# Experts' tiles of a routed mixture layer: three engines' programs turned from unrolled code into loops of four tiles

## The reference, cut to what matters

```python
logits = xt @ Wr + br                       # 4096 tokens of 128 values, 8 experts
top_p, top_idx = jax.lax.top_k(softmax(logits), 2)
xe = xn[None] * ln_g[:, None] + ln_b[:, None]
h = gelu(einsum('end,edh->enh', xe, W1) + b1[:, None], approximate=False)
y = einsum('enh,ehd->end', h, W2) + b2[:, None]
out = sum over the two chosen experts of weight * y
```

## Time and profile before

| | |
|---|---|
| median of the timed runs | 1002.8 us |
| the profiled execution, its span | 1045.3 us |
| share of the span by PE, DVE, ACT, POOL | 73%, 70%, 61%, 56% |
| matmuls | 7837 |
| instructions executed | 24181 |
| first tile's tokens to last tile's results | about 867 to 1007 us of the span |
| TensorE's granted clock there, in mid-stage | 1.00 |

### The profile page before, as it was taken

The page is one execution under the profiler, slowest core; times in us unless marked ns, Lnnn a source line. Parts: engine busy times, 40 slices in busy tenths (PEclk is TensorE's granted clock), DMA queues, the critical chain, the costliest instruction groups (busy, mean ns, idle before and its releaser), DMA issues. The chain is left out here.

```text
span 1045.3 us, 24181 instructions
## 1 busy us (share of the span) xinstructions
PE 761.2 (73%) x7837; PEld 473.6 (45%) x7837; DVE 729.2 (70%) x1821; ACT 641.5 (61%) x1446; POOL 587.3 (56%) x760
## 2 busy tenths in 40 slices
PE   2857888888888888888888599665554306899960
PEld 2444444444454454444544244212443305777750
DVE  2585788888888888888887715697745543666646
ACT  2656888887888888888888332285322404777740
POOL 0045777767767767767767499200065561555560
PEclk8896999999999999999999699888655557999995
DMA  9009999980000000000000050130011112222317
GB/s 218 1 2 203 172 187 118 6 3 0 0 0 0 0 0 0 0 0 0 0 0 0 4 159 1 55 126 3 1 41 41 33 44 60 64 83 73 83 47 241
DMA packets 109052, 54.07 MB, mean 52 GB/s; under 512 B 42688, under 2 KB 100824, under 8 KB 109008
## 3 DMA queue, kind: packets, MB, share of 16 engines
q1 hardware_dynamic: 102624, 43.34, 27.5%
q0 software_dynamic: 4544, 9.38, 2.8%
q10 hardware_dynamic: 1840, 0.79, 0.4%
HBM read 21.49 MB, written 29.44 MB: 49 GB/s over the span
## 5 line engine op out<-in xcount | busy, mean ns | idle before, releaser
L534 DVE SCALAR_TENSOR_TENSOR l_m<-l_m,l_eta,lp_g 128x256 f32<-128x256 f32 x512 | 219.6, 476 | 39.5 <-PE lp_g L646 26.0
L383 POOL TENSOR_TENSOR s_w<-l_kw,l_m 128x512 f32<-128x512 f32 x192 | 238.4, 1278 | 12.0 <-DVE l_m L534 12.0
L480 ACT ACTIVATE l_kw<-s_w,l_keep_lr 128x256 f32<-128x256 f32 x384 | 171.3, 507 | 0.0
L1338 POOL DMA_INDIRECT f_yg<-f_yr,f_xmeta x78 | 78.7, 1009 | 75.1 <-DVE f_yr L1668 55.9
L1333 POOL DMA_INDIRECT f_xg<-f_xrow,f_place x64 | 62.9, 983 | 74.7 <-DVE f_place L1564 56.4
L1313 ACT ACTIVATE f_hh<-fp_v,f_bcol 128x256 f32<-128x256 f32 x156 | 63.2, 480 | 33.4 <-PE fp_v L1433 32.4
L473 ACT COPY l_wt<-lp_b 128x512 f32<-128x512 f32 x96 | 56.4, 588 | 27.8 <-PE lp_b L639 27.8
L388 POOL TENSOR_TENSOR l_kw<-s_w,l_keep 128x512 f32<-128x512 f32 x64 | 65.2, 1040 | 0.0
L639 PE MATMUL lp_b<-s_cst,s_w 128*128 128x128 f32 x384 | 62.7, 287 | 2.3 <-ACT s_w L521 1.3
L1433 PE MATMUL fp_v<-f_xf,s_w_hi 128*128 128x256 bf16 x312 | 56.0, 281 | 9.3 <-DVE f_xmeta L1648 7.2
L639 PEld LDWEIGHTS lp_b<-s_cst,s_w 128*128 128x128 f32 x384 | 43.7, 143 | 32.5 <-ACT l_wt L473 13.8
(11 more groups left out here) (323 smaller groups left out, 2016.4 us busy)
## 6 DMA issues: line engine op xcount, KB each, us to landing
f_xg<-s_pad SPq DMA_DIRECT2D x1, 17280.0 KB, 106.7
f_xt<-f_xg SPq DMA_DIRECT2D x39, 130.0 KB
r_w<-in_L_ffn_W_dram SPq DMA_DIRECT2D x16, 256.0 KB, 3.1
s_w<-f_yg SPq DMA_DIRECT2D x16, 256.0 KB, 3.7
xs<-in_x_dram SPq DMA_DIRECT2D x8, 256.0 KB, 7.5
t_w<-in_L_ffn_W_dram SPq DMA_DIRECT2D x8, 256.0 KB
out_dram<-s_x SPq DMA_DIRECT2D x8, 256.0 KB, 3.0
s_xsh<-s_xl SPq DMA_DIRECT2D x4, 448.0 KB, 3.5
```

The lines of the kernel that those rows point to most:

```text
L383: nc.gpsimd.tensor_tensor(W[k][:, half(h), :], KW[k][:, half(h), :], M[k][:, half(h), :], ALU.add).then_inc(w_ready[k], 1)
L480: m = nc.scalar.mul(KW[k][:, b, :], W[k][:, b, :], keep_lr[:, b:b + 1])
L534: i = nc.vector.scalar_tensor_tensor(out=M[k][:, b, :], in0=M[k][:, b, :], scalar=eta[:, b:b + 1], in1=ps_g[b][:, 0:256], op0=ALU.mult, op ...
L1338: nc.gpsimd.indirect_dma_start(sb["yg"][:, :], bass.IndirectOffsetOnAxis(ap=xmeta[:, j, a, 0:1].bitcast(mybir.dt.int32), axis=0), yr[j % R ...
```

## The change

`RING` becomes 4. The fourth `f_hs` buffer, and all four of `f_yr`, are placed in the memory of `s_qf`, which is no longer used. The programs of TensorE, ScalarE and VectorE for the tiles are written as a helper `rounds`: tiles 0 to 5 stand written out, then a hardware loop of 8 rounds with four tiles in its body, then the rest (tile 38, and on TensorE and VectorE the two steps that drain the pipeline). Within the loop the number of the tile is a register expression, `at(r, k)`, so the numbers that are waited for, the column of `owneri` and the offsets of biases and of `xmeta` are computed in registers. TensorE reads the tile's owner twice, once for the first and once for the second layer, where before it kept the register. SyncE's and GpSimd's programs stay written out, with the ring of four. The order of the matmuls, activations and copies is as before. ScalarE's wait for a free `f_hs` buffer is for the second layer of three tiles ago as before; VectorE's is for that of four tiles ago.

```diff
-    RING = 3
+    RING = 4
+    AHEAD, ROUNDS = 6, 8
...
+        def at(r, k, n=1):
+            return r * (RING // n) + k // n
+
+        def rounds(engine, step, last):
+            for k in range(AHEAD):
+                step(0, k)
+            with engine.Fori(0, ROUNDS) as r:
+                for k in range(RING):
+                    step(r, AHEAD + k)
+            for k in range(AHEAD, last - RING * ROUNDS):
+                step(ROUNDS, k)
...
-                    if j >= 2:
-                        act.wait_ge(h_lo, 2 * (j - 1))
+                def activated(r, k):
+                    if k >= 2:
+                        act.wait_ge(h_lo, 2 * at(r, k - 1))
...
-                def owner_of(j):
-                    return nc.tensor.value_load(owner_i[0:1, j:j + 1], min_val=0, max_val=E - 1)
+                def owner_of(r, k):
+                    return nc.tensor.value_load(owner_i[0:1, bass.ds(at(r, k), 1)], min_val=0, max_val=E - 1)
...
+                def first_layer(r, k, e):
+                    pe.wait_ge(xf_ready, 2 * at(r, k) + 2)
+                    if k >= 2:
+                        pe.wait_ge(h_ready, NH * at(r, k - 1))
...
+                def layers(r, k):
+                    if RING * ROUNDS * (r is ROUNDS) + k + 1 < NJ:
+                        turn(r, k + 1)
+                    if RING * ROUNDS * (r is ROUNDS) + k < NJ:
+                        first_layer(r, k, owner_of(r, k))
+                    if k >= 2:
+                        second_layer(r, k - 2, owner_of(r, k - 2))
...
-                for j in range(NJ + 2):
-                    if j + 1 < NJ:
-                        turn(j + 1)
-                    if j < NJ:
-                        e = owners[j] = owner_of(j)
...
-                        e = owners.pop(i)
-                        pe.wait_ge(h_lo, 2 * (i + 1))
...
+                rounds(pe, layers, NJ + 2)
```

More of the change, by code:

```diff
@@ L1185, in experts @@
         spare = sb["qf"][:, :, :, :].rearrange("p b t c -> p (b t c)")
-        hs.append([spare[:, 512 * i:512 * i + 512].bitcast(BF16).rearrange("p (h n) -> p h n", h=NH) for i in range(2)])
-        yr = [buf(f"yr{i}", [128, 2, 128]) for i in range(RING)]
+        for n in range(2):
+            hs.append([spare[:, 1024 * n + 512 * i:1024 * n + 512 * i + 512].bitcast(BF16).rearrange("p (h n) -> p h n", h=NH) for i in range(2)])
+        yr = [spare[:, 2048 + 256 * i:2304 + 256 * i].rearrange("p (a n) -> p a n", a=2) for i in range(RING)]
         yb = [sb["w" + k][:, :, :].rearrange("p b n -> p (b n)").rearrange("p (k n f) -> p k n f", k=2, n=4) for k in ("10", "11", "21")]
@@ L1228, in tile_of, with plain @@
             return NTB * (i % B) + 2 * g + i // B
+        def at(r, k, n=1):
[8 more added lines that the diff above has]
+                step(ROUNDS, k)
+        def plain(step, last):
+            for k in range(last):
+                step(0, k)
         with nc.Block() as block:
@@ L1306, in _ @@
                 act.wait_ge(owner_ready, 4)
-                for j in range(NJ):
-                    if j >= 2:
-                        act.wait_ge(h_lo, 2 * (j - 1))
+                def activated(r, k):
+                    if k >= 2:
+                        act.wait_ge(h_lo, 2 * at(r, k - 1))
                     for h in range(NH):
                         if h % 2 == 0:
[L1312 to L1316, removed]
+                            act.wait_ge(h_done, 2 * at(r, k) + h // 2 + 1)
+                        nc.scalar.activation(hh[k % 2][:, h, :], ps_h[k % 2][:, SL * h:SL * h + SL], ACT.Gelu,
+                                             bias=bcol[:, h, bass.ds(at(r, k), 1)]).then_inc(h_ready, 1)
+                    if k >= 3:
+                        act.wait_ge(y_done, at(r, k - 2))
                     for p in range(2):
-                        act.wait_ge(h_ready, NH * j + 2 * p + 2)
-                        nc.scalar.copy(hs[j % 3][0][:, 2 * p:2 * p + 2, :], hh[j % 2][:, 2 * p:2 * p + 2, :]).then_inc(h_hi, 1)
+                        act.wait_ge(h_ready, NH * at(r, k) + 2 * p + 2)
+                        nc.scalar.copy(hs[k % RING][0][:, 2 * p:2 * p + 2, :], hh[k % 2][:, 2 * p:2 * p + 2, :]).then_inc(h_hi, 1)
+                rounds(act, activated, NJ)
             @block.gpsimd
@@ L1398, in _, with turn @@
                     counts(g)
[L1400 to L1404, removed]
+                def turn(r, k):
+                    pe.wait_ge(xt_in[k % RING], 16 * at(r, k, RING) + 16)
+                    if k >= 2:
+                        pe.wait_ge(xf_ready, 2 * at(r, k - 1))
                     for i in range(4):
-                        m = nc.tensor.transpose(ps_xb[j % 2][:, 128 * i:128 * i + 128], xt[j % RING][:, i % 2, 128 * (i // 2):128 * (i // 2) + 128], identb[:, :])
+                        m = nc.tensor.transpose(ps_xb[k % 2][:, 128 * i:128 * i + 128], xt[k % RING][:, i % 2, 128 * (i // 2):128 * (i // 2) + 128], identb[:, :])
                     m.then_inc(xt_turned, 1)
@@ L1410, in chosen @@
                     return w[:, bass.ds(e, 1), 128 * h:128 * h + 128].rearrange("p a n -> p (a n)")
-                def owner_of(j):
-                    return nc.tensor.value_load(owner_i[0:1, j:j + 1], min_val=0, max_val=E - 1)
-                owners = {}
+                def owner_of(r, k):
[4 more added lines that the diff above has]
+                        pe.wait_ge(h_ready, NH * at(r, k - 1))
+                    for h in range(NH):
+                        p = ps_h[k % 2][:, SL * h:SL * h + SL]
+                        for n, (b, c) in enumerate(PRODUCTS):
+                            m = nc.tensor.matmul(p, chosen(w1s[b], e, h), xf[k % 2][:, c, :], start=n == 0, stop=n == 2)
+                        if h % 2 == 1:
+                            m.then_inc(h_done, 1)
@@ new lines, in second_layer @@
+                def second_layer(r, k, e):
+                    pe.wait_ge(h_lo, 2 * at(r, k) + 2)
+                    if k == 1:
+                        pe.wait_ge(owner_ready, 4)
+                    if k >= 2:
+                        pe.wait_ge(y_ready, at(r, k - 1))
+                    for h in range(NH):
+                        w = w2b[:, bass.ds(e, 1), h, :, :].rearrange("p a c n -> p (a c n)")
+                        for a in range(2):
+                            p = ps_y[k % 2][:, 256 * a:256 * a + 256]
+                            nc.tensor.matmul(p, hs[k % RING][0][:, h, 128 * a:128 * a + 128], w, start=(a, h) == (0, 0), stop=False)
+                            nc.tensor.matmul(p[:, 0:128], hs[k % RING][1][:, h, 128 * a:128 * a + 128], w[:, 0:128], start=False, stop=False)
+                    m = nc.tensor.matmul(ps_y[k % 2].rearrange("p (a n) -> p a n", a=2)[:, :, 0:128], mine[:, bass.ds(at(r, k), 1)].to_broadcast([128, 128]),
+                                         btab[:, H:H + 128].rearrange("p (a n) -> p a n", a=1).to_broadcast([128, 2, 128]), start=False, stop=True)
+                    m.then_inc(y_done, 1)
@@ L1420, in _ @@
                 m.then_inc(table_done, 1)
-                turn(0)
-                for j in range(NJ + 2):
-                    if j + 1 < NJ:
-                        turn(j + 1)
-                    if j < NJ:
-                        e = owners[j] = owner_of(j)
[L1427 to L1437, removed]
-                        e = owners.pop(i)
-                        pe.wait_ge(h_lo, 2 * (i + 1))
[L1440 to L1452, removed]
+                turn(0, 0)
+                rounds(pe, layers, NJ + 2)
             @block.vector
@@ L1650, in _, with arrive @@
[L1650 to L1668, removed]
+                def arrive(r, k):
+                    dve.wait_ge(xt_turned, at(r, k) + 1)
+                    if k >= 2:
+                        dve.wait_ge(h_done, 2 * at(r, k - 1))
+                    nc.vector.tensor_copy(xf[k % 2][:, :, :].rearrange("p a n -> p (a n)"), ps_xb[k % 2][:, 0:512]).then_inc(xf_ready, 1)
+                    nc.vector.tensor_copy(xmeta[:, bass.ds(at(r, k), 1), :, :].rearrange("p j a c -> p (j a) c"), tile[k % RING][:, :, 128:130]).then_inc(xf_ready, 1)
@@ new lines, in remainders, with summed @@
+                def remainders(r, k):
+                    if k >= 4:
+                        dve.wait_ge(y_done, at(r, k - 3))
+                    for p in range(2):
+                        dve.wait_ge(h_hi, 2 * at(r, k) + p + 1)
+                        nc.vector.tensor_tensor(hs[k % RING][1][:, 2 * p:2 * p + 2, :], hh[k % 2][:, 2 * p:2 * p + 2, :],
+                                                hs[k % RING][0][:, 2 * p:2 * p + 2, :], ALU.subtract).then_inc(h_lo, 1)
+                def summed(r, k):
+                    dve.wait_ge(y_done, at(r, k) + 1)
+                    if k >= RING:
+                        dve.wait_ge(yr_free[k % RING], 32 * at(r, k, RING))
+                    dve.wait_ge(xf_ready, 2 * at(r, k) + 2)
+                    parts = ps_y[k % 2].rearrange("p (a c n) -> p a c n", a=2, c=2)
```

(10 more changed lines are left out.)

7 lines of the change are left out of this document (1 added, 6 removed).

## The result

| | median of the timed runs | ratio to the kernel before, 95% interval |
|---|---|---|
| before | 1003.2 us | |
| changed | 1026.7 us | 1.0226, 1.0200 to 1.0253 |
| changed, timed again later | 1029.7 us | 1.0277, 1.0233 to 1.0322 |

The direction was forecast, the size was not: +23 us where +10 stood, and the time lies 0.7 us above the range. All ratios leave out runs far from the others (in the first experiment one of 2304 us, and one of the kernel before of 1450 us). The profiled execution of the changed kernel has a span of 1023.2 us, shorter than the 1045.3 of the profile before. So by the two profiles the change gains 22 us, and by the timed runs it loses 23. One of the profiles doesn't tell of the timed runs, and the first experiment shows which.

The account below looks back on a forecast made before the run. TensorE was nearest to full; after the change its sequencer would set the pace. Loop +6.7, outside tiles +0.5, late news +3.2 made +10.4 us on 1045.3, scaled to +10 on 1002.8: 1012.8 us, range 989 to 1026.

Parts of the forecast that it names:

- TensorE's sequencer would set the time: In the tile loop, added reads and register operations exceed the 0.46 us to spare; slower, 1012.8 us, chance 0.58.
- The sequencer's tile after the change, 3.7 us (3.35 to 3.85): TensorE's sequencer per loop tile: 2.5 + 0.65 second read + 0.5 register operations + 0.06 loop end.
- The tile before, 3.49 us: Mid-stage pace read from the 1045.3 us profile, 10.48 us for three tiles; gave +6.7 us over 32 tiles.
- Late news after the change, +3.2: TensorE's late news of finished matmuls still costs 0.1 us a tile in the loop; bounds 0 to +17 us.
- Seven tiles outside of the loop, +0.5: Tiles written out get only the second read: 3.15 us against the array's 2.96; bounds 0 to +1.3 us.
- The other engines' register operations and the fourth buffers, 0: ScalarE's and VectorE's register operations are hidden but for 0.3 us counted under late news; no wait for a free buffer.
- Rival 1: Faster: program loads hold up TensorE's news and a loop that stays loaded ends that; 992 us, chance 0.25.
- the hold: TensorE's late news of finished matmuls, 1.6 us once in three tiles; GpSimd's scatter held likelier than program loads, two to one.
- Rival 2: The same: sequencer's tile of 3.4 to 3.55 us traded for the loss of the hold; 1001 to 1004.8 us, chance 0.11.
- Rival 3: Much slower: each turn of the loop loads its program anew, two loads in each of 8 rounds; 1028 us, chance 0.06.
- the learning loop: Another loop in the kernel, 440 us, 31 branches of 0.21 us without instruction DMA; cited against reloading in each turn.
- What would show it: Profile signs: loop tiles 3.6 to 3.9 us apart, 0.5 us "issue" gap before second layers, TensorE about 0.8 busy.

Follow-up runs that it names:

- the first experiment: The kernel before, with no edit, run and profiled again: ratio 1.0015 (0.9997 to 1.0033), profiled span 1003.7 us, 2.96 us a tile.
- second profile of before: Second profiled execution of the unedited kernel before: span 1003.7 us, 2.96 us a tile, against 1045.3 us in its first profile.
- The loop of 1451: The changed kernel with two turns of 16 tiles in place of eight of 4, owner read twice: 3.59 us a tile, ratio 1.0197.

## Why the prediction was wrong in size

Point by point, by its steps:

- **TensorE's sequencer would set the time.** Right, by the reads added one by one, by TensorE's loop alone, and by the removal of the second read and of the range check, after which the loss is gone.
- **The sequencer's tile after the change, 3.7 us (3.35 to 3.85).** Right: 3.71. Its parts are 2.59 for 2.5 before, 0.64 for 0.65 of the read, 0.13 for 0.06 of the loop's end, and the 0.35 that is left for 0.5 of register operations. The misses cancel, which is luck. The five register operations already held the loop's own three in four tiles, so its end was in part counted twice.
- **The tile before, 3.49 us.** This is the step that failed: "In the loop, 32 tiles: 32 x (3.7 - 3.49) = +6.7 us". The timed runs have 2.96. With that, 32 x (3.71 - 2.96) = +24 us. So the cost that was added was sized rightly, and what it was held against was not. I had the 2.96 from the earlier trace rows as the array's need, and used the drawn-out pace as what is lost today. "The timed runs are 4% shorter than this execution, and nothing shows that the stage is shorter by more" was wrong too. The stalls I had found were of the size of what the span had too much: 1.6 us in each three tiles, and 4 to 5 us a piece ahead of the stage, beside 42.5. I read them as something the kernel does, and should have asked first whether an execution that long can tell what the timed ones do.
- **Late news after the change, +3.2.** Measured 0: there is no hold in either profile of the changed kernel. This term moved the forecast toward the measured time without a cause in it.
- **Seven tiles outside of the loop, +0.5.** From the first tile's activation to the last tile's are 137.3 us after and 111.3 in the second profile of before, +26.0. Less 24 for the loop, some 2 are left. The tiles ahead of the loop, from the third on, stand at 3.14 to 3.28 us, as one more read makes them (3.23).
- **The other engines' register operations and the fourth buffers, 0.** Right, by the run with TensorE written out.
- **Rival 1** needed a sequencer's tile under 3.49 and the program's loads as the cause of the hold. The tile is 3.71, and 13 loads came without a hold; so did the scatters, which I held for the likelier cause. **Rival 2** needed a tile of 3.4 to 3.55 and the hold in the timed runs; neither is so. **Rival 3**, a turn that loads its program anew: 4 loads in the whole stage, none in a later turn. What was held against it, the learning loop, was weak: that loop has some 365 instructions a turn, one block and a half. The loop of 1451 is the test.
- **The range.** The bounds of the three terms add up to -4.5 and +29.8 us, scaled some 998 to 1031. The 1004 to 1028 given for this case isn't their sum, and 1026 as the range's end cut it shorter still. The measured 1027 lies inside the added bounds only by the late news' upper end, +17, which did not come.
- **What would show it.** The gap ahead of each second layer was forecast at 0.5 us and is 0.44 on the chain below; the tiles' distance, the two reads a tile and the four blocks on the queue came as forecast; TensorE's busy share fell to 0.88 and not to 0.8, but from 1.00 and not from 0.91; ScalarE's long wait beside a scatter did not appear.

Where a tile's 0.8 us go is best seen on the two chains of waits, second profile of before, then after (start us, us, what):

```profile
907.79 1.31 PE fp_v L1433 x12
909.10 0.11 PE fp_y L1448
...
910.42 0.11 PE fp_y L1450
910.53 0.22 PE fp_x L1406 x4
910.76 1.31 PE fp_v L1433 x12
```

```profile
909.38 1.48 PE fp_v L1446 x12
910.87 0.44 issue
911.30 0.28 PE fp_y L1460
...
912.79 0.11 PE fp_y L1462
912.90 0.22 PE fp_x L1430 x4
913.17 1.48 PE fp_v L1446 x12
```

From the first layer's start to the second's are 1.31 us before and 1.92 after: the queue of matmuls runs empty (0.44 of "issue") while the sequencer reads the owner, 0.65 us, and does the register operations behind it. These two tiles differ by 0.82 us. Beside the 0.44, 0.17 each stand at the first and at the second layer, whose first matmul counts in full behind a gap (1.48 for 1.31, 0.28 for 0.11), and 0.04 behind the transposes.

## What to carry to other kernels

An engine at 100% busy hides its sequencer only up to the time of its own work: count control operations per tile at some 0.12 us each, the step in the earlier trace rows, with 0.65 us for the three of a checked read, and compare the sum with the array's time before a loop adds to it. As an estimate this gives 15 x 0.12 + 0.65 = 2.45 us for the kernel before (2.59 by the runs) and 20 x 0.12 + 2 x 0.65 = 3.7 for the changed one (3.71). If the profiled execution is longer than the timed runs, profile again before a stall in it is put into a sum; if one stretch of it shows the bare pace of the bounding engine, take that for the timed kernel as a rival at least. A value that two steps of a loop need belongs in a register that lives across turns; here this and dropping the range check took back the 23 us together. With the check kept, 3.71 - 0.64 = 3.07 us a tile would be left by the prices above, an estimate that no run tried.

## What the runs showed of the hardware

- A checked read of a value into TensorE's sequencer costs 0.64 us where the sequencer is the bound: 0.36 for the load, 0.21 for the operation of 151 ns behind it, 0.08 for the assertion. Unchecked it is 0.36 and some 0.1. The floor of 0.6 us that the prediction weighed from the Trainium skill ("DMA: Bandwidth & Descriptors", Latency and other measured facts) doesn't hold for this load: by it, 3.23 us would have been 3.5.
- The turn of a loop costs TensorE's sequencer 0.5 us, more than twice its branch's own 0.21; an operation of register arithmetic among matmuls costs about 0.08, by what is left over (0.35 us for 4.25 operations).
- A loop of 1451 instructions on TensorE was loaded once, 8 blocks in all with what lies around it, and its second turn loaded none. The Trainium skill ("Runtime: NRT & Kernel Launch", Instruction fetch mechanics) gives TensorE room for 2048 instructions and, on the same page, a window of two pages of 256 outside of which a taken branch stops the sequencer. This trace agrees with the first and not with the second. The learning loop, which the prediction named, can't decide the second: two such pages can hold its 365 instructions.
- One execution in which TensorE's news of finished matmuls came late from about 765 us on, some 41 us in all, was met once in thirteen profiles. The loads of its program are not the cause (nine of thirteen waits have none in them); nothing in the trace names another.
